# A graph network and expert kernel on one core: GpSimd takes over the whole split of level 0's weights

## The chip, the cores and the metric

One core of a Trainium2 chip. The time is that of one execution on the device, in microseconds (us).

## The reference

A graph network of three levels on 625 nodes of 256 features, followed by a layer of 8 experts. What matters here is the first of them:

```python
def _edge_conv(x, src, dst, W, b):
    xi = x[dst]
    xj = x[src]
    m = jnp.concatenate([xi, xj - xi], axis=-1) @ W + b
    s = jax.ops.segment_sum(m, dst, num_segments=N)
    cnt = jax.ops.segment_sum(jnp.ones((dst.shape[0],), m.dtype), dst, num_segments=N)
    return s / jnp.maximum(cnt, 1.0)[:, None]
...
for W, b in ((W0, b0), (W1, b1), (W2, b2)):
    h = jax.nn.relu(_edge_conv(h, src, dst, W, b))
    xs.append(h)
cat = jnp.concatenate(xs, axis=-1)
return cat @ Wf + bf
```

There are 20,000 edges, sorted by their target. x goes through a layernorm first. W has two halves: one for a node's own row (xi) and one for its neighbour minus itself. Since the sum over edges is linear, a level is (upper half of W minus lower half) applied to the own row times the node's degree, and the lower half applied to the neighbours' rows, added up through a 625 x 625 matrix of edge counts.

## The kernel before

One program writes out the instructions of each engine by hand, with semaphores between them. Five things run in its first 41 us.

**The matrix of edge counts.** The edges are taken in 40 units of 500. VectorE makes two tables of zeros and ones for each pair of units (`hot_pair`, lines 991 to 1004: `hot_lo` at L997 and `hot_key` at L1000, each comparing a constant table in SBUF with the edges' numbers in SBUF). TensorE multiplies them into a pane in PSUM (`sum_unit`, L1434 to L1444), and ScalarE copies each pane to its place in `a_hi` or `a_f` (`write_pair`, L724). Where a new pair of tables may overwrite an old one, VectorE waits for TensorE. TensorE's pairs of units are its `sum_pair(12)` to `sum_pair(38)`, with other products written in between them by hand (L1476 to L1508).

**The layernorm.** VectorE takes statistics of x (`bn_stats` L1013, `bn_aggr` L1016), ScalarE the square root, VectorE three Newton steps (L1024 to L1028), ScalarE writes the rows (`xn_row`, L739). TensorE transposes them (L1469), ScalarE rounds them to float32r (`ht_upper`, L746 to L750) and VectorE takes what rounding lost (`ht_lower`, L1046 to L1050).

**Level 0's weights.** W0 (two halves) and the first part of Wf are loaded to `w_stage` by SyncE (L485, L487). Every weight that a product uses is split into an upper half, rounded to float32r (`w_hi`), and a lower half, the rest (`w_lo`), so that three products give float32 precision (`exact3`, L1383). Parts 0, 1 and 2 are the neighbours' half, the difference of the two halves, and Wf's part. For level 0 VectorE makes the difference (L1036, in place), ScalarE the three upper halves (`w_upper`, L743) and VectorE the three lower halves (`w_lower`, L1041). The semaphore `w_split` counts 1 when parts 0 and 1 are there and 2 when part 2 is. TensorE waits for 1 before its first product with the weights (L1485, `ys_product`, L1406), together with `ht_ready`, and for 2 before the product with Wf at the end of level 0 (L1621). SyncE waits for 2 before it loads W1 into the same `w_stage` (L507).

**The later weights.** GpSimd makes the difference (L614) and the lower halves (L620) for level 1 with ScalarE's upper halves (L842), behind a wait for all additions of the adjacency (`a_added`, VectorE L1091) and for the load; for level 2 and the end it makes everything (`split_weights`, L574: difference L584, upper halves L587, lower halves L591). TensorE's levels 1 and 2 wait for counts 3 and 4 of `w_split` (L1615).

**GpSimd's queue** is: constants to L572; then a wait for `span_read` and `max_read` and four tiny operations on the ranges of the chunks (L603 to L606, `flagged`), which decide whether a general path is taken (not here); then a wait for all layernorm rows and a DMA that adds bf to x (L610); then the level 1 work.

SyncE's queue loads, in order, the edges, x, W0 and Wf's part, biases, the 16 blocks of expert weights, then (behind `w_split`) W1 and the rest.

Of the kernel before, what the change touches and what calls it, by code (L numbers as in the profile page):

```python
# [8 lines left out]
D = 256  # L9
# [84 lines left out]
def build(nc, x, src, dst, W, B, Wf, bf, Wg, bg, W1, b1, W2, b2, out):  # L94
    f32, f32r = mybir.dt.float32, mybir.dt.float32r
    bf16, i32, i16, u32 = mybir.dt.bfloat16, mybir.dt.int32, mybir.dt.int16, mybir.dt.uint32
    ALU = mybir.AluOpType
# [5 lines left out]
    with ctx:  # L103
        def sb(name, shape, dt, scope=ctx):
            return scope.enter_context(nc.sbuf_tensor(name, shape, dt))

        def sem(name):
            return ctx.enter_context(nc.semaphore(name))
# [35 lines left out]
        w_stage = sb("w_stage", [P, 3, KC, D], f32, gnn)  # L144
        w_hi = sb("w_hi", [P, 2, KC, 3 * D], f32r, gnn)
        w_lo = sb("w_lo", [P, 2, KC, 3 * D], f32r, gnn)
# [114 lines left out]
        w_in = [sem(f"w_in{l}") for l in range(LEVELS + 1)]  # L261
# [7 lines left out]
        w_split = sem("w_split")  # L269
# [16 lines left out]
        tables = sem("tables")  # L286
        base_ready = sem("base_ready")
        a_zeroed = sem("a_zeroed")
        w_diffed = sem("w_diffed")
        w_hi_done = sem("w_hi_done")  # L290
        w1_diffed = sem("w1_diffed")
        w1_hi_done = sem("w1_hi_done")
        hot_made = sem("hot_made")
# [179 lines left out]
        def edge_cols(a):  # L473

            return bank[3 + a][0:EP, 0:ET].rearrange("p (j q) -> p q j", j=EH)
# [63 lines left out]
        def _(pool):  # L539
# [34 lines left out]
            def split_weights(l):  # L574
# [15 lines left out]
                for i, part in parts:  # L590
# [5 lines left out]
                pool.sem_inc(w_split, 1)  # L596


            pool.wait_ge(span_read, 2)
            pool.wait_ge(max_read, 2)  # L600
            pool.wait_ge(consts, 5)
# [4 lines left out]
            pool.tensor_scalar(flags[:, 2 * CHUNKS - 2:], lo[:, SPLIT_CHUNK:SPLIT_CHUNK + 2], -1.0,  # L606
                               float(SPLIT - 1), ALU.mult, ALU.add).then_inc(flagged, 1)

            pool.wait_ge(xn_ready, NT)
            pool.dma_start(x_sb[:], bf.unsqueeze(0).unsqueeze(0).broadcast_to((P, NT, D)), accum_op=ALU.add)\  # L610
                .then_inc(bf_added, 16)
# [78 lines left out]
        def _(act):  # L690
# [26 lines left out]
            def chunk_starts(a):  # L717

                _, starts = nc.values_load_multi_w_load_instructions(
                    base_i[0:1, a:a + 8], engines=(mybir.EngineType.Activation,), min_val=0, max_val=NODES - 1,  # L720
                    skip_runtime_bounds_check_because="the least of a chunk's node numbers, which are below NODES")
                return starts

            def write_pair(g, a, starts):  # L724
                for k in (a, a + 1):
                    act.wait_ge(pane_done, k + 1)
                    if k >= 2:
                        act.wait_ge(a_written, k - 1)
                    act.copy((a_hi, a_f)[k % 2][:, :, ds(starts[k - a], TURN_W[g])],
                             pane(k).rearrange("p (n w) -> p n w", n=NT)).then_inc(a_written, 1)  # L730
# [9 lines left out]
                act.activation(xn[:, t, :], x_sb[:, t, :], ACT.Identity, bias=shift[:, t:t + 1], scale=rstd[:, t:t + 1])\  # L740
                    .then_inc(xn_ready, 1)

            def w_upper(i):  # L743
                act.copy(w_hi[:, 0, :, i * D:(i + 1) * D], w_stage[:, (1, 0, 2)[i], :, :]).then_inc(w_hi_done, 1)

            def ht_upper(i):  # L746
                (h, c) = Z_OUT[i]
                act.wait_ge(xn_t_done, i + 1)
                a, b = HALVES[h]
                act.copy(ht_hi[:, c, a:b], xn_bank(i)).then_inc(ht_hi_done, 1)  # L750
# [23 lines left out]
            write_pair(0, 6, starts[6:8])  # L774
            act.wait_ge(edge_col_done, 3)
            act.copy(edge_key[:].rearrange("p (q j) -> p q j", j=EH), edge_cols(1)).then_inc(edge_key_done, 1)
            act.wait_ge(w_in[0], 32)
            w_upper(0)
            starts = chunk_starts(8)
            write_pair(1, 8, starts[0:2])  # L780
            act.wait_ge(rstd_ready, 1)
# [4 lines left out]
            xn_row(2)  # L786
            write_pair(1, 14, starts[6:8])
            starts = chunk_starts(16)
            act.wait_ge(w_diffed, 1)
            w_upper(1)  # L790
            write_pair(1, 16, starts[0:2])
            xn_row(3)
            write_pair(1, 18, starts[2:4])
# [9 lines left out]
            ht_upper(2)  # L803
            ht_upper(3)
            write_pair(2, 28, starts[4:6])
            w_upper(2)
            write_pair(2, 30, starts[6:8])
            key_table(4)
            def write_units(g, u):
# [131 lines left out]
        def _(dve):  # L941
            n = [0]

            def mark(ins):
                n[0] += 1
                ins.then_inc(vec, 1)

            def wait_marked():
                dve.wait_ge(vec, n[0])

            def chain(ins):
                mark(ins)
                wait_marked()
# [61 lines left out]
            for t in range(NT):  # L1015
# [16 lines left out]
            dve.wait_ge(tables, 3)  # L1032
            dve.wait_ge(edge_col_done, 3)
            hot_pair(4)
            dve.wait_ge(w_in[0], 32)
            dve.tensor_tensor(w_stage[:, 0, :, :], w_stage[:, 0, :, :], w_stage[:, 1, :, :], ALU.subtract)\  # L1036
                .then_inc(w_diffed, 1)
            hot_pair(5)
            hot_pair(6)

            def w_lower(i):  # L1041
                dve.wait_ge(w_hi_done, i + 1)
                return dve.tensor_tensor(w_lo[:, 0, :, i * D:(i + 1) * D], w_stage[:, (1, 0, 2)[i], :, :],
                                         w_hi[:, 0, :, i * D:(i + 1) * D].bitcast(f32), ALU.subtract)

            def ht_lower(i):  # L1046
                (a, b), c = HALVES[Z_OUT[i][0]], Z_OUT[i][1]
                dve.wait_ge(ht_hi_done, i + 1)
                dve.tensor_tensor(ht_lo[:, c, a:b], xn_bank(i), ht_hi[:, c, a:b].bitcast(f32),
                                  ALU.subtract).then_inc(ht_ready, 1)  # L1050

            hot_pair(7)
            dve.wait_ge(tables, 4)
            w_lower(0)
            hot_pair(8)
            w_lower(1).then_inc(w_split, 1)
            ht_lower(0)
            ht_lower(1)
            hot_pair(9)
# [3 lines left out]
            hot_pair(11)  # L1063
            dve.wait_ge(tables, 5)
            hot_pair(12)
            w_lower(2).then_inc(w_split, 1)

            dve.wait_ge(flagged, 1)
            chain(dve.tensor_reduce(meta[:], flags[:], AX.X, ALU.max))
# [707 lines left out]
```

## Time and profile before

| | us |
|---|---|
| median of 3 runs | 165.92 (164.61 to 166.39) |
| the profiled execution | 165.11 |
| its span | 163.3 |
| TensorE, matmuls busy | 138.1 (85%) |
| VectorE busy | 88.6 (54%) |
| GpSimd busy | 65.6 (40%) |
| ScalarE busy | 63.8 (39%) |

The span is what the profiler saw of the core; about 1.8 us of the execution lie around it. PE is TensorE, PEld its loading of weights, DVE VectorE, ACT ScalarE, POOL GpSimd, SP SyncE; SPq and the like are an engine's queue. L12 is line 12 of the kernel. Busy shares are averages over stages that have different limits, so they don't tell what a change in one stage is worth. The spans of GpSimd instructions are rough. Names drop digits and buffer numbers (`w_stage`, `bank`). Consecutive instructions of an engine overlap a little in a timeline.

### The profile page before, as it was taken

What the parts mean: (1) busy time and instruction counts of PE and PEld (TensorE: products, weight loads), DVE (VectorE), ACT (ScalarE), POOL (GpSimd) and SP (SyncE); (2) the same over time, 40 slices, a digit from 0 to 9 for tenths busy, and PEclk for the clock granted to TensorE, in tenths of its full rate; (3) what the DMA queues carried; (4) which work ended last, traced back from release to release, by engine and by line L of the source; (5) the groups of instructions that cost most, each with busy time, mean ns of one, the idle gap of its engine ahead of it and who ended that gap; (6) DMA issues with size and microseconds to landing.
All of it is one profiled execution on the core that took longest, in us unless ns stands there. A gap on an engine that the chain in (4) does not pass through costs nothing.

```text
span 163.3 us, 3291 instructions
## 1 busy us (share of the span) xinstructions
PE 138.1 (85%) x1093; PEld 128.2 (79%) x1094; DVE 88.6 (54%) x251; ACT 63.8 (39%) x214; POOL 65.6 (40%) x78
## 2 busy tenths in 40 slices
PE   1432779998999999999999998887999999999800
PEld 1322659988998999999999987877999899999600
DVE  6799999789479980445048887641232223321110
ACT  7517895577172131322131480322443333333200
POOL 5805040000089099930000300058466867844531
PEclk9999999999999999999999999999999999999995
DMA  4959999799301910200000632012344434452322
GB/s 121 289 148 381 368 368 290 146 285 366 121 3 35 370 62 0 68 4 0 0 0 4 190 107 90 0 32 66 65 68 64 66 64 68 72 91 34 34 32 32
DMA packets 15770, 18.80 MB, mean 115 GB/s; under 512 B 1666, under 2 KB 13220, under 8 KB 15620
## 3 DMA queue, kind: packets, MB, share of 16 engines
q1 hardware_dynamic: 12692, 14.71, 27.8%
q0 software_dynamic: 3056, 3.80, 14.6%
q8 instruction: 13, 0.21, 0.6%
q14 instruction: 9, 0.07, 0.1%
HBM read 15.25 MB, written 3.26 MB: 113 GB/s over the span
## 4 chain that ended last, share of the span: by engine, by line
PE 73%; DVE 14%; issue 4%; DMA 3%; ACT 1%; POOL 1%; DVEq 1%; POOLq 0%; ACTq 0%
PE cnt_ps L1713 13%; PE bank L1699 8%; PE bank L1523 6%; PE g_ps L1699 6%; PE cnt_ps L1523 5%; PE g_ps L1387 3%; PE g_ps L1386 3%; PE g_ps L1388 3%; DVE hot_lo L997 3%; PE g_ps L1442 3%; PE bank L1442 3%; PE cnt_ps L1386 2%; PE bank L1386 2%; PE cnt_ps L1387 2%; PE cnt_ps L1388 2%
## 5 line engine op out<-in xcount | busy, mean ns | idle before, releaser
L660 POOL DMA_INDIRECT out_rows<-y_sb,row_of x13 | 20.6, 1585 | 15.9 <-SPq L533 9.1
L1331 DVE TENSOR_TENSOR y_sb<-cnt_ps,b_bc 128x256 f32<-128x256 f32 x13 | 5.5, 425 | 36.5 <-PE cnt_ps L1713 36.5
L1713 PE MATMUL cnt_ps<-w_sb,h_t 128*128 x104 | 24.7, 380 | 0.7 <-DVE y_sb L1331 0.7
L1713 PEld LDWEIGHTS cnt_ps<-w_sb,h_t 128*128 128x128 f32 x104 | 18.7, 190 | 3.1 <-issue 1.1
L654 POOL DMA_INDIRECT xg<-x_rows,row_of x11 | 12.9, 1176 | 18.7 <-DVE row_of L1364 15.7
L1699 PE MATMUL bank<-xt,w_fix 128*128 128x128 f32 x112 | 13.8, 276 | 1.2 <-DVE w_fix L1317 1.2
L1699 PEld LDWEIGHTS bank<-xt,w_fix 128*128 128x128 f32 x112 | 13.1, 191 | 2.2 <-DVE w_fix L1317 1.6
L911 ACT ACTIVATE h_t<-bank,b_col 128x128 f32<-128x128 f32 x28 | 8.0, 369 | 16.6 <-PE bank L1699 16.6
L997 DVE TENSOR_TENSOR hot_lo<-iota_lo,edge_rel 125x1024 bf16<-125x1024 int16 x20 | 13.8, 688 | 1.2 <-PE g_ps L1442 1.1
L1442 PE MATMUL bank<-hot_key,hot_lo 125*128 125x45 bf16 (+4 forms) x80 | 8.4, 245 | 5.5 <-DVE hot_key L1000 4.1
L911 ACT ACTIVATE h_t<-g_ps,b_col 128x128 f32<-128x128 f32 x24 | 6.9, 370 | 13.9 <-PE g_ps L1699 13.9
L1699 PEld LDWEIGHTS g_ps<-xt,w_fix 128*128 128x128 f32 x96 | 11.2, 192 | 0.9 <-issue 0.4
L1699 PE MATMUL g_ps<-xt,w_fix 128*128 128x128 f32 x96 | 11.8, 276 | 0.0
L1442 PEld LDWEIGHTS bank<-hot_key,hot_lo 125*128 125x128 bf16 x80 | 5.3, 125 | 8.0 <-DVE hot_key L1000 5.7
L614 POOL TENSOR_TENSOR w_stage<-w_stage 128x512 f32<-128x512 f32 x1 | 1.3, 1297 | 23.2 <-DMA w_stage<-in_L_gnn_Wf 23.2
L1442 PE MATMUL g_ps<-hot_key,hot_lo 125*128 125x45 bf16 (+4 forms) x80 | 8.5, 245 | 2.0 <-DVE hot_key L1000 1.8
L1317 DVE COPY w_fix<-w_sb 128x1024 f32 x13 | 9.2, 710 | 0.7 <-DVE in L1314 0.7
L1523 PE MATMUL bank<-a_hi,ys_hi 128*128 128x384 f32 (+1 forms) x30 | 9.1, 316 | 0.0
L1523 PE MATMUL bank<-a_hi,ys_lo 128*128 128x384 f32 (+1 forms) x30 | 9.0, 316 | 0.0
L1188 DVE SCALAR_TENSOR_TENSOR ut_lo<-bank,ut_hi 128x384 fp32r<-128x384 f32 x4 | 2.2, 558 | 12.5 <-ACT ut_hi L882 12.5
L762 ACT CAST ys_hi<-ys_f 128x256 fp32r<-128x256 f32 x10 | 4.1, 409 | 12.4 <-DVE ys_f L1084 12.4
L1000 DVE TENSOR_TENSOR hot_key<-key_tables,edge_rel 125x360 bf16<-125x360 int16 (+4 forms) x20 | 8.9, 445 | 0.0
(288 smaller groups left out, 379.0 us busy)
## 6 DMA issues: line engine op xcount, KB each, us to landing
w_sb<-in_L_ffn_W SPq DMA_DIRECT2D x16, 512.0 KB, 9.1
w_stage<-in_L_gnn_W SPq DMA_DIRECT2D x3, 512.0 KB, 4.8
w_stage<-in_L_gnn_Wf SPq DMA_DIRECT2D x4, 256.0 KB, 5.5
b_bc<-in_L_ffn_b SPq DMA_DIRECT2D x1, 1024.0 KB, 6.0
x_sb<-in_L_gnn_bf POOLq DMA_DIRECT2D x1, 640.0 KB, 15.0
x_rows<-x_f SPq DMA_DIRECT2D x1, 640.0 KB, 3.3
x_sb<-in_x SPq DMA_DIRECT2D x1, 512.0 KB
out_rows<-x_sb SPq DMA_DIRECT2D x1, 512.0 KB
```

Of the source, the lines that this page charges most:

```text
L654: pool.indirect_dma_start(out=xg[:, b, :], out_offset=None, in_=x2_rows, in_offset=bass.IndirectOffsetOnAxis(ap=rows, axis=0)).then_inc(x_ ...
L660: pool.indirect_dma_start(out=out, out_offset=bass.IndirectOffsetOnAxis(ap=rows, axis=0), in_=y_sb[:, b, :], in_offset=None, compute_op=AL ...
L911: last = act.activation(h_t[:, h, k, :], up_bank(h)[:, k * P:(k + 1) * P], ACT.Gelu, bias=b1_col[:, ds(e, 1), k:k + 1])
L997: dve.tensor_tensor(hot_lo[:, u % RING:u % RING + 2, :, :], iota_lo[0:EP].unsqueeze(1).broadcast_to((EP, 2, P, CT)), rel[:, 0].unsqueeze(2 ...
L1000: dve.tensor_tensor(hot_keys(u, 2), turn_keys(u // UNROLL)[0:EP].rearrange("p n w i -> p (n w) i").unsqueeze(1) .broadcast_to((EP, 2, NT * ...
L1317: dve.tensor_copy(w1_fix[:, h, :, :], w1_sb[:, ds(e, 1), :, :]).then_inc(w1_placed, 1)
L1386: pe.matmul(out_, lh, rh, start=first, stop=False, skip_group_check=True)
L1387: pe.matmul(out_, lh, rl, start=False, stop=False, skip_group_check=True)
L1442: last = pe.matmul(pane(k), hot_lo[:, u % RING, :, i], hot_keys(u)[:, 0, :, i], start=i == i0, stop=i == i0 + n_i - 1, skip_group_check=True)
L1523: step = pe.matmul(o, y[:, u, m], a_t[:, u, cols], start=first and u == 0 and y is y_parts[0], stop=u == NT - 1 and y is y_parts[-1], skip ...
L1699: last = pe.matmul(up_bank(h)[:, j * P:(j + 1) * P], w1_fix[:, h, k, j * P:(j + 1) * P], xt[:, k, h * P:(h + 1) * P], start=j == 0 and k == 0,
L1713: last = pe.matmul(bank[3][:, 0:D], h_t[:, h, k, :], w2_sb[:, ds(e, 1), k, :], start=k == 0, stop=k == HC - 1)
```

## The change

GpSimd makes the difference, the three upper halves and the three lower halves of level 0. Its new instructions stand between the constants and the four operations on the ranges (difference, parts 0 and 1), and between those and the DMA of bf (part 2). Each one waits for the one before it (`chain`). ScalarE's three copies and VectorE's four instructions go, with the two semaphores between them.

```diff
@@ gpsimd @@
+            def w_part(i):
+                return w_stage[:, (1, 0, 2)[i], :, :]
+
+            def w_lower(i):
+                return pool.tensor_tensor(w_lo[:, 0, :, i * D:(i + 1) * D], w_part(i),
+                                          w_hi[:, 0, :, i * D:(i + 1) * D].bitcast(f32), ALU.subtract)
+
+            pool.wait_ge(w_in[0], 32)
+            chain(pool.tensor_tensor(w_stage[:, 0, :, :], w_stage[:, 0, :, :], w_stage[:, 1, :, :], ALU.subtract))
+            for i in range(2):
+                chain(pool.tensor_copy(w_hi[:, 0, :, i * D:(i + 1) * D], w_part(i)))
+                chain(w_lower(i))
+            pool.sem_inc(w_split, 1)
             pool.wait_ge(span_read, 2)
             pool.wait_ge(max_read, 2)
...
+            chain(pool.tensor_copy(w_hi[:, 0, :, 2 * D:], w_part(2)))
+            chain(w_lower(2))
+            pool.sem_inc(w_split, 1)
             pool.wait_ge(xn_ready, NT)
@@ scalar @@
-            def w_upper(i):
-                act.copy(w_hi[:, 0, :, i * D:(i + 1) * D], w_stage[:, (1, 0, 2)[i], :, :]).then_inc(w_hi_done, 1)
-
...
-            act.wait_ge(w_in[0], 32)
-            w_upper(0)
...
-            act.wait_ge(w_diffed, 1)
-            w_upper(1)
...
-            w_upper(2)
@@ vector @@
             hot_pair(4)
-            dve.wait_ge(w_in[0], 32)
-            dve.tensor_tensor(w_stage[:, 0, :, :], w_stage[:, 0, :, :], w_stage[:, 1, :, :], ALU.subtract)\
-                .then_inc(w_diffed, 1)
             hot_pair(5)
             hot_pair(6)
-
-            def w_lower(i):
-                dve.wait_ge(w_hi_done, i + 1)
-                return dve.tensor_tensor(w_lo[:, 0, :, i * D:(i + 1) * D], w_stage[:, (1, 0, 2)[i], :, :],
-                                         w_hi[:, 0, :, i * D:(i + 1) * D].bitcast(f32), ALU.subtract)
...
             hot_pair(7)
             dve.wait_ge(tables, 4)
-            w_lower(0)
             hot_pair(8)
-            w_lower(1).then_inc(w_split, 1)
             ht_lower(0)
             ht_lower(1)
...
             hot_pair(12)
-            w_lower(2).then_inc(w_split, 1)
```

## Rows read from the trace of the kernel before

**Rows 1.** The page, part 2: busy tenths in 40 slices of 4.08 us.
```profile
PE   1432779998999999999999998887999999999800
DVE  6799999789479980445048887641232223321110
```

**Rows 2.** The chain of waits, 10 to 25 us: start us, us, what.
```profile
10.82 0.60 DVE hot_lo L997
...
14.67 0.74 DVE w_stage L1036
...
17.00 0.29 DVE hot_key L1000
...
21.29 0.56 DVE ht_lo L1049
...
24.74 0.37 PE bank L1386
```

**Rows 3.** Timeline of VectorE, 13 to 24.5 us; groups of ScalarE, 9 to 25 us.
```profile
14.59 0.82 DVE L1036 TENSOR_TENSOR w_stage<-w_stage 128x512 f32<-128x512 f32 x1
15.33 0.79 DVE L997 TENSOR_TENSOR hot_lo<-iota_lo,edge_rel 125x1024 bf16<-125x1024 int16 x1
...
16.32 0.68 DVE L997 TENSOR_TENSOR hot_lo<-iota_lo,edge_rel 125x1024 bf16<-125x1024 int16 x1
...
18.08 0.68 DVE L1043 TENSOR_TENSOR w_lo<-w_stage,w_hi 128x512 fp32r<-128x512 f32 x1
...
20.70 1.15 DVE L1049 TENSOR_TENSOR ht_lo<-cnt_ps,ht_hi 128x384 fp32r<-128x384 f32 x2 [0.39 <-ACT ht_hi L750]
...
L744 ACT CAST w_hi<-w_stage 128x512 fp32r<-128x512 f32 x3 | 1.9, 628 | 0.4 <-issue 0.4
```

**Rows 4.** Timeline of GpSimd, 12 to 24 us.
```profile
13.80 0.64 POOL L603 TENSOR_TENSOR over<-span_bc,limit 1x72 f32<-1x72 f32 x1 [5.98 <-issue]
14.52 0.34 POOL L604 TENSOR_TENSOR flags<-over,span_bc 1x72 f32<-1x72 f32 x1
...
20.61 1.76 POOL L610 DMA_DIRECT2D x_sb<-in_L_gnn_bf  x1 [4.44 <-ACT x_sb L740]
```

**Rows 5.** DMA issues, 0 to 14 us (last number: us to landing); SyncE's timeline.
```profile
w_stage<-in_L_gnn_Wf SPq DMA_DIRECT2D x1, 256.0 KB, 5.5
...
3.50 0.50 SPq L487 DMA_DIRECT2D w_stage<-in_L_gnn_Wf  x1
...
33.46 2.67 SPq L485 DMA_DIRECT2D w_stage<-in_L_gnn_W  x1
```

**Rows 6.** Timeline of GpSimd, 36 to 100 us.
```profile
45.61 1.30 POOL L614 TENSOR_TENSOR w_stage<-w_stage 128x512 f32<-128x512 f32 x1 [23.24 <-DMA w_stage<-in_L_gnn_Wf]
...
68.79 0.61 POOL L587 CAST w_hi<-w_stage 128x512 fp32r<-128x512 f32 x1
```

**Rows 7.** Timelines of VectorE and GpSimd, 49 to 66 us.
```profile
49.21 2.19 DVE L1188 SCALAR_TENSOR_TENSOR ut_lo<-z,ut_hi 128x384 fp32r<-128x384 f32 x2
...
49.39 1.60 POOL L620 TENSOR_TENSOR w_lo<-w_stage,w_hi 128x512 fp32r<-128x512 f32 x1
...
58.83 0.43 DVE L1078 TENSOR_TENSOR ys_lo<-ys_f,ys_hi 128x256 fp32r<-128x256 f32 x1
...
60.20 0.56 DVE L1078 TENSOR_TENSOR ys_lo<-ys_f,ys_hi 128x256 fp32r<-128x256 f32 x1 [0.19 <-ACT ys_hi L762]
...
65.21 0.56 DVE L1188 SCALAR_TENSOR_TENSOR ut_lo<-bank,ut_hi 128x384 fp32r<-128x384 f32 x1 [4.45 <-ACT ut_hi L882]
```

**Rows 8.** Timelines, 38 to 53 us; a stretch (its 1.00: granted clock); the chain.
```profile
38.57 4.11 DVE L1091 TENSOR_TENSOR a_hi<-a_hi,a_f 128x384 fp32r<-128x384 f32 x10
...
52.12 0.44 PE L1386 MATMUL bank<-ut_hi,w_hi 128*128 128x384 f32 x1 [0.22 <-issue]
...
24.50:30.80 6.30, 6.30 (x47) 6.02 (x46) 5.66 (x14) 3.59 (x18) 0.00 (x0) 1.00 0.99 240
...
27.06 0.21 PE cnt_ps L1387
...
32.75 0.12 PE cnt_ps L1387
```

More of the change, by code:

```diff
@@ L288, in build @@
         a_zeroed = sem("a_zeroed")
-        w_diffed = sem("w_diffed")
-        w_hi_done = sem("w_hi_done")
         w1_diffed = sem("w1_diffed")
```

## The prediction, made before the change was run

> **What bounds the kernel now.** The page comes first. Its digits by slice [rows 1] show TensorE low in the first six slices (0 to 24.5 us) and high later, and VectorE high from the start to 24.5 us: the change lies in the stretch where VectorE leads and TensorE waits. Who ends the waits is in the chain of waits, cut to 10 to 25 us [rows 2]: it runs along VectorE from hot_lo at 10.82 us to hot_key at 17.00, the difference of level 0's weights (14.67) among it, then over TensorE's transposes and ScalarE's ht_hi to VectorE's ht_lo (21.29), its next hot tables, and back to TensorE, which at 24.74 is in the first weight product. From there TensorE is dense. So a microsecond on VectorE before 20 us moves the start of the dense part by nearly a microsecond, and most of the span behind it is that dense part.
>
> **What goes.** VectorE loses four instructions. In its timeline [rows 3] the difference takes 15.33 - 14.59 = 0.74 us from start to start; the first lower half has 0.68, of which 0.08 overlaps its neighbour (14.59 + 0.82 against 15.33 is the same overlap), so 0.60; the second, of the same form, 0.60 too. These three stand ahead of ht_lo: 1.94 us. The third lower half stands behind the start of the dense part, where hot tables are made ahead of need: I value it at nothing, at most its 0.60 us. ScalarE loses three copies of 0.63 us [rows 3], two of them ahead of ht_hi. What ScalarE handles there (panes, layernorm rows) comes from VectorE's tables and scale, so I count no gain beyond VectorE's; but where VectorE gets faster, these 1.26 us keep ScalarE from being late in its place. VectorE waits 0.39 us for ht_hi ahead of ht_lo [rows 3]: so much of a gain, or of a loss, is swallowed there. With nothing else in play the first weight product would come 1.94 - 0.39 = 1.55 us earlier.
>
> **What comes, on GpSimd.** It has been idle for 5.98 us when its first flag operation starts at 13.80 [rows 4], so it is free from 7.8 us. The last part of W0's load is issued at 3.50 us and lands 5.5 us later, at 9.0 us [rows 5]; the wait wants all of it, so the work begins at 9.0. One difference or lower half alone takes 1.30 us, one copy to the upper half 0.61 us [rows 6]. Difference, upper 0, lower 0, upper 1, lower 1 are 3 x 1.30 + 2 x 0.61 = 5.1 us; the four waits on itself at some 0.1 us each (13.80 + 0.64 to 14.52 in rows 4 is such a gap) make 5.5 us: alone it ends at 14.5. TensorE asks for it at 24.5: as work it is well hidden. Behind it in GpSimd's queue stand four small flag operations, which only feed meta, read after VectorE's hot_pair(12); then upper 2 and lower 2 (2.0 us), wanted by the product with Wf at the end of level 0; then the DMA that adds bf, which waits for the last layernorm row anyway (20.61 [rows 4]) and whose result is read only after that product. None of these is near its user. SyncE waits for the second count of w_split before it loads W1, but its queue gets there only at 33.46 us [rows 5]; the count is then there in both kernels.
>
> **What it does to VectorE.** This term decides. The trace has one clean place where a GpSimd lower half meets VectorE instructions with two SBUF inputs: the two ut_lo at 49.21 [rows 7]. The form alone takes 0.56 us, a pair 2 x 0.56 - 0.08 = 1.04; here the pair took 2.19 us, and the lower half 1.60 in place of 1.30. The second ut_lo stood until GpSimd was done: 2.19 - 1.04 = 1.15 us for VectorE. A copy does the same, though the row shows only its tail: ys_lo at 60.20, behind a copy, took 0.56 us, the one at 58.83 took 0.43 [rows 7]. And in the very stretch of this change the tiny flag operations lengthened the difference (0.82 against 0.68 for the same form at 18.08) and hot_lo at 15.33 (0.79 against 0.68 at 16.32) [rows 3], and were stretched themselves: 0.64 and 0.34 us for one shape [rows 4]. hot_lo and hot_key read two SBUF inputs and follow each other without a gap: a GpSimd instruction gets in behind the running one, and the next stands for its time.
>
> In order: the difference (9.0 to 10.3) lies beside bn_stats, bn_aggr, a reduction and span_diag, which have one input tensor each and last to hot_lo at 10.82: nothing (if they do stand, 1.15 more). Upper 0 (10.4 to 11.0) reaches over 10.82: 0.2 us. Lower 0, between hot_lo and hot_key: 1.15. Upper 1, shorter than its duration by as much as the lower half: 0.61 - 0.15 = 0.46. Lower 1, at the Newton steps and hot_pair(3): 1.15. Upper 2 and lower 2, behind the flags and among hot_pair(5) to (8): 0.46 and 1.15. Sum 0.2 + 3 x 1.15 + 2 x 0.46 = 4.57 us of standing. Against it 1.94 saved and 0.39 swallowed: 4.57 - 1.94 - 0.39 = 2.24 us later at the first weight product. The bounds: below, no standing at all, a gain of 1.55; above, each instruction's whole duration and the difference too, 0.2 + 4 x 1.30 + 2 x 0.61 = 6.62, so 6.62 - 1.94 - 0.39 = 4.29 later. I take 2.24: ut_lo met exactly the instruction that is added, and the rows from 13.8 to 16 us show the same with hot_lo itself.
>
> The Trainium skill speaks against this change. In "SBUF — State Buffer", section "Who interferes with whom", it says that a VectorE instruction with two SBUF inputs contends with a GpSimd instruction that reads SBUF, and under "SBUF: two separate sides" that the loser is blocked for the whole instruction. The two ut_lo agree in kind; by whole durations in place of 1.15 and 0.46 the sum would be 0.2 + 3 x 1.30 + 2 x 0.61 - 1.94 - 0.39 = 3.0 us. The measured pair is what my sum goes by.
>
> **What the shift meets later.** The dense part moves as a whole. A gain would meet a gate: level 1 waits for the third count of w_split, given at 49.39 + 1.60 = 50.99 us [rows 7], and TensorE starts level 1 at 52.12 [rows 8]; GpSimd begins that work at 45.6, when W1's load has landed [rows 6], at the end of a full DMA queue. So 1.1 us of a gain pass at most. A delay finds that gate early: the other condition of the work, VectorE's last addition of the adjacency (38.57 + 4.11 = 42.68 [rows 8]), has 2.9 us to spare. The delay passes whole.
>
> TensorE's clock: the granted clock stands at 1.00 throughout [rows 8], but one step of a 256-column product takes 0.21 us at 27.06 and 0.12 at 32.75 [rows 8]: the pace of 1.2, then of 2.4 GHz. If the pace comes up at the same time of the run though the dense part begins 2.24 us later, 2.24 x (1 - 0.12 / 0.21) = 0.96 us are won back; if it falls out of step the other way, as much is lost. I take it in step.
>
> The profiled execution has 165.11 us, the median of the three shown 165.92. The sum on the first is 165.11 + 2.24 = 167.35; the forecast is for such a median, 165.92 + 2.24 = 168.2 us.
>
> **The rivals.**
> 1. VectorE's relief wins, which ends on the faster side: 165.92 - 1.1 = 164.8 us. Place: 9 to 20 us; it decides if the standing is below 1.94 us, under 0.4 for each of the five instructions that meet hot tables. For it: both relieved engines are busy there, and GpSimd has ten us to spare. Against it: the 2.19 us pair. Chance 0.10.
> 2. The standing is there but partly won back: TensorE's pace comes up at the same time, 168.2 - 0.96 = 167.2, or with 0.5 us more on instructions that read one tensor, 166.7 us. For it: VectorE has such instructions up to 10.8 us. Against it: hot tables are most of its time afterwards. Chance 0.25.
> 3. Heavier: whole durations, or GpSimd starting late. Its first tensor_tensor now comes at 13.80 behind idleness that the trace puts down to nothing ("issue"); if that hides something the engine needs, the difference too falls among the hot tables: 165.92 + 4.29 = 170.2 at worst, 168.9 by whole durations alone. Chance 0.17.
> The forecast as it stands has 0.48.
>
> **How the numbers follow.** A change within 1% (1.66 us) is about what a measurement of this kernel can't tell from none. The forecast lies 2.24 us above; of its 0.48 some 0.09 falls within 1%, of rival 2's 0.25 some 0.16, of rival 1 half (0.05; the other half if the gate lets more pass than I read), of rival 3 nothing. That makes faster 0.05, within 1% 0.30, slower 0.65. The range leaves out rival 1 and rival 3's far end: 165.9 to 169.9 us.
>
> **What would show it.** Right: GpSimd's difference starts near 9.0 us, ahead of the flags; in five places between 10.8 and 22 us a hot_lo of 0.68 or a small step behind a GpSimd instruction grows by 0.5 to 1.15 us; the first weight product starts near 26.8 us in place of 24.6, and what is behind it is later by the same. Wrong: hot_lo stays at 0.68 beside GpSimd's instructions and the product starts before 24.5 us (rival 1); the product is 2 us late but the span is not (rival 2: the pace, or slack behind that I didn't see); the difference starts after 10.8 us (rival 3). If W1's work or bf's DMA ended a wait on the path, my reading of the queues would be wrong.

## The result and the profile after

Twenty executions of each kernel: before 165.07 us in the median (164.25 to 166.41), after 166.00 (165.66 to 167.25). The ratio is 1.0058, 95% interval 1.0039 to 1.0076: slower by 0.93 us in the median, clear of noise, where 2.24 were forecast. The profiled execution of after has 165.9 us (span 164.1), that of before 165.11 (163.3). On another chip, timed again at the end, the same kernel gave 1.0085 (1.0053 to 1.0117). There the medians differ by 1.30 us. Both intervals hold 1.0053 to 1.0076. So the direction was right and the time lies in the range given, at its low end, but the size is less than half of the forecast's. (The forecast's base, 165.92, was the median of three executions and lies 0.85 above that of twenty, so the differences are what can be compared.)

The first weight product starts at 26.22 us in place of 24.55, 1.67 later. The page's part 2 of after, which answers to [rows 1], shows GpSimd busy in the third and fifth slices (8.2 to 12.2 and 16.3 to 20.4 us), where it did nothing in before, and VectorE about as busy as before, its standing counted as busy. The last row is before's:

```profile
PE   1413489998999999999999998897999999999800
DVE  6799999879659990346037887632222233321110
...
POOL 5886940000149279960000300057467766854531
```

```profile
POOL 5805040000089099930000300058466867844531
```

GpSimd's timeline of after, 8 to 24 us (start us, us, instruction), answers to [rows 4]:

```profile
8.68 1.26 POOL L605 TENSOR_TENSOR w_stage<-w_stage 128x512 f32<-128x512 f32 x1 [0.78 <-DMA w_stage<-in_L_gnn_Wf]
10.00 0.61 POOL L607 CAST w_hi<-w_stage 128x512 fp32r<-128x512 f32 x1
10.69 1.26 POOL L601 TENSOR_TENSOR w_lo<-w_stage,w_hi 128x512 fp32r<-128x512 f32 x1
12.02 1.33 POOL L607 CAST w_hi<-w_stage 128x512 fp32r<-128x512 f32 x1
13.42 1.26 POOL L601 TENSOR_TENSOR w_lo<-w_stage,w_hi 128x512 fp32r<-128x512 f32 x1
...
18.24 0.96 POOL L620 CAST w_hi<-w_stage 128x512 fp32r<-128x512 f32 x1
19.28 1.28 POOL L601 TENSOR_TENSOR w_lo<-w_stage,w_hi 128x512 fp32r<-128x512 f32 x1
```

VectorE's timeline of after over the same stretch answers to [rows 3]; the rows of before behind it show the small operations undisturbed:

```profile
10.12 0.51 DVE L1024 TENSOR_SCALAR var_eps<-mv 128x5 f32<-128x5 f32 x1
...
10.98 1.03 DVE L1026 TENSOR_SCALAR span_diag<-ident,span 80x80 f32<-80x80 f32 x1
...
12.54 0.33 DVE L1006 TENSOR_TENSOR hot_key<-key_tables,edge_rel 125x360 bf16<-125x360 int16 x1
...
13.00 0.36 DVE L1031 TENSOR_TENSOR newton<-rstd 128x5 f32<-128x5 f32 x1
...
13.59 1.11 DVE L1033 SCALAR_TENSOR_TENSOR rstd<-newton,rstd 128x5 f32<-128x5 f32 x1
...
16.92 0.82 DVE L1003 TENSOR_TENSOR hot_lo<-iota_lo,edge_rel 125x1024 bf16<-125x1024 int16 x1
...
18.65 0.77 DVE L1006 TENSOR_TENSOR hot_key<-key_tables,edge_rel 125x400 bf16<-125x400 int16 x1
19.34 1.77 DVE L1003 TENSOR_TENSOR hot_lo<-iota_lo,edge_rel 125x1024 bf16<-125x1024 int16 x1
...
22.39 1.14 DVE L1047 TENSOR_TENSOR ht_lo<-cnt_ps,ht_hi 128x384 fp32r<-128x384 f32 x2
```

```profile
10.05 0.17 DVE L1018 TENSOR_SCALAR var_eps<-mv 128x5 f32<-128x5 f32 x1
...
10.56 0.26 DVE L1020 TENSOR_SCALAR span_diag<-ident,span 80x80 f32<-80x80 f32 x1
...
11.81 0.17 DVE L1025 TENSOR_TENSOR newton<-rstd 128x5 f32<-128x5 f32 x1
...
12.21 0.17 DVE L1027 SCALAR_TENSOR_TENSOR rstd<-newton,rstd 128x5 f32<-128x5 f32 x1
```

Read the two engines side by side. `span_diag` starts at 10.98 and ends at 12.01, when the lower half that began at 10.69 is over (11.95). `rstd`, a 0.17 us operation, ends at 14.70, the second lower half at 14.68. `hot_lo` at 19.34 takes 1.77 us: it stands until the third lower half is over (20.56), then needs its 0.6. Each of these VectorE instructions begins under a GpSimd one and stands until that one ends. Not every one does: `bn_stats`, `bn_aggr`, the reduction and the reciprocal keep their durations beside GpSimd, and where a hot table is under way it can be GpSimd that is held: its copy at 12.02 takes 1.33 us in place of 0.61, while `hot_key` at 12.54 keeps its 0.33. VectorE's standing, over the durations of before: 0.34 + 0.77 + 0.19 + 0.94 = 2.24 us ahead of `hot_pair(4)`'s end and 0.42 + 1.09 = 1.51 behind it, 3.75 in all (4.57 forecast).

For what follows I take two points. P is the start of VectorE's instruction behind `hot_pair(4)`: 14.59 in before [rows 3], 16.92 in after. H is the start of the first `ht_lo`: 20.70 and 22.39. From H to the first weight product it is 3.83 to 3.85 us in all traces but one. So P is 2.33 later, P to H is 5.47 in place of 6.11, and the product is 2.33 - 0.64 = 1.69 later, as the row says within 0.02.

### The profile page after: what moved, and what is told of

It reads as the page before. It is cut to its first block, busy times and chain, and to the rows that moved or that the text cites. A ratio compares the mean times of both kernels' runs of the same rounds, so it can differ in the third digit from the quotient of the medians.

```text
span 164.1 us, 3293 instructions
## 1 busy us (share of the span) xinstructions
PE 137.1 (84%) x1093; PEld 127.6 (78%) x1094; DVE 89.9 (55%) x247; ACT 62.5 (38%) x211; POOL 72.5 (44%) x85
## 4 chain that ended last, share of the span: by engine, by line
PE 68%; DVE 22%; issue 4%; DMA 1%; ACT 1%; POOL 1%; DVEq 1%; POOLq 0%; ACTq 0%
PE cnt_ps L1708 14%; PE bank L1694 8%; PE g_ps L1694 7%; PE cnt_ps L1518 5%; PE bank L1518 4%; DVE hot_lo L1003 3%; PE g_ps L1381 3%; PE bank L1437 3%; PE g_ps L1382 3%; PE g_ps L1383 3%; PE g_ps L1437 2%; PE cnt_ps L1381 2%; DVE hot_key L1006 2%; PE bank L1381 2%; PE cnt_ps L1382 2%
## 5 line engine op out<-in xcount | busy, mean ns | idle before, releaser
L1708 PE MATMUL cnt_ps<-w_sb,h_t 128*128 x104 | 24.7, 380 | 0.7 <-DVE y_sb L1326 0.7
L668 POOL DMA_INDIRECT xg<-x_rows,row_of x11 | 12.1, 1104 | 18.7 <-DVE row_of L1359 15.7
L1003 DVE TENSOR_TENSOR hot_lo<-iota_lo,edge_rel 125x1024 bf16<-125x1024 int16 x20 | 14.9, 743 | 1.1 <-PE g_ps L1437 1.1
L628 POOL TENSOR_TENSOR w_stage<-w_stage 128x512 f32<-128x512 f32 x1 | 1.3, 1284 | 20.4 <-DMA w_stage<-in_L_gnn_Wf 20.4
L1006 DVE TENSOR_TENSOR hot_key<-key_tables,edge_rel 125x360 bf16<-125x360 int16 (+4 forms) x20 | 9.4, 470 | 0.0
L1437 PEld LDWEIGHTS g_ps<-hot_key,hot_lo 125*128 125x128 bf16 x80 | 6.0, 122 | 3.8 <-DVE hot_key L1006 3.2
```

The lines of the kernel that those rows point to most:

```text
L668: pool.indirect_dma_start(out=xg[:, b, :], out_offset=None, in_=x2_rows, in_offset=bass.IndirectOffsetOnAxis(ap=rows, axis=0)).then_inc(x_ ...
L1003: dve.tensor_tensor(hot_lo[:, u % RING:u % RING + 2, :, :], iota_lo[0:EP].unsqueeze(1).broadcast_to((EP, 2, P, CT)), rel[:, 0].unsqueeze(2 ...
L1006: dve.tensor_tensor(hot_keys(u, 2), turn_keys(u // UNROLL)[0:EP].rearrange("p n w i -> p (n w) i").unsqueeze(1) .broadcast_to((EP, 2, NT * ...
L1437: last = pe.matmul(pane(k), hot_lo[:, u % RING, :, i], hot_keys(u)[:, 0, :, i], start=i == i0, stop=i == i0 + n_i - 1, skip_group_check=True)
L1708: last = pe.matmul(bank[3][:, 0:D], h_t[:, h, k, :], w2_sb[:, ds(e, 1), k, :], start=k == 0, stop=k == HC - 1)
```

## The experiments

My theory after the result: it is GpSimd's reading of SBUF that makes VectorE stand, and the part of it ahead of P sets the product's lateness, while between P and H the work is not VectorE's alone. Rivals: GpSimd being busy at all is enough; the relief or the standing behind P counts too; the whole is an effect of when TensorE's pace rises. A table first; "product" and "span" are of the one trace, the ratio is against before on the same chip.

| kernel | P | P to H | product | span | ratio (95%) |
|---|---|---|---|---|---|
| before, two traces | 14.59, 14.68 | 6.11, 6.11 | 24.55, 24.63 | 163.3, 162.5 | |
| after, three traces | 16.92, 17.00, 17.55 | 5.47, 5.47, 5.49 | 26.22, 26.30, 26.88 | 164.1, 164.3, 164.5 | 1.0058; 1.0085 |
| reading instructions added | 16.54 | 6.89 | 27.14 | 164.9 | 1.0143 (1.0110 to 1.0175) |
| writing ones added | 14.94 | 6.11 | 24.89 | 164.0 | 0.9999 (0.9969 to 1.0029) |
| difference alone moved | 14.65 | 5.81 | 24.31 | 162.9 | 0.9990 (0.9969 to 1.0010) |
| part 2 given back | 17.19 | 5.49 | 26.52 | 163.9 | 1.0084 (1.0051 to 1.0117) |
| VectorE delayed | 16.99 | 6.09 | 26.93 | 164.8 | 1.0135 (1.0098 to 1.0172) |
| after, a copy's time on ScalarE | 17.15 | 5.81 | 26.80 | 164.6 | 1.0086 (1.0052 to 1.0120) |
| upper 0 and 1 early | 15.74 | 5.16 | 24.75 | 162.2 | 0.9979 (0.9954 to 1.0003) |
| the same, part 2 late | 14.66 | 5.18 | 23.67 | 162.7 | 0.9997 (0.9970 to 1.0025) |

### Seven GpSimd instructions added that read

Against before; the scratch tile is 128 x 2 x 512 and feeds nothing. They stand where the change puts its own.

```diff
+        scr = sb("scr", [P, 2, KC, D], f32, gnn)
...
+            chain(pool.memset(scr[:, 0, :, :], 1.0))
+            pool.wait_ge(w_in[0], 32)
+            def ex(short):
+                if short:
+                    chain(pool.tensor_copy(scr[:, 1, :, :], scr[:, 0, :, :]))
+                else:
+                    chain(pool.tensor_tensor(scr[:, 1, :, :], scr[:, 0, :, :], scr[:, 0, :, :], ALU.subtract))
+            ex(0)
+            for i in range(2):
+                ex(1)
+                ex(0)
             pool.wait_ge(span_read, 2)
...
+            ex(1)
+            ex(0)
             pool.wait_ge(xn_ready, NT)
```

> The kernel before, unchanged in what it computes, plus GpSimd work of the form and at the place of the change (four subtractions and three copies of 128x512, on a scratch tile, each waiting for the one before; one memset of 0.5 us ahead). VectorE and ScalarE keep all their instructions. Theory P (VectorE stands while GpSimd reads SBUF): nothing is saved, so the first weight product comes by the whole standing, 3.8 us in the changed kernel's trace, less VectorE's 0.39 us of slack: about 3.4 us after 24.55, and the time is 2.3 to 3.4 us longer. Rival Q (the time comes from GpSimd's own lateness: its flags and the DMA of bf behind the new work): the same lateness is there, so about 0.9 us longer, and hot tables of 0.68 us stay 0.68.

166.99 against 164.81 us, 1.0143. ScalarE and VectorE keep all their work here, so this is the price of GpSimd's instructions alone. VectorE's timeline:

```profile
11.99 0.79 DVE L1039 TENSOR_TENSOR newton<-rstd 128x5 f32<-128x5 f32 x1
...
13.01 0.46 DVE L1041 SCALAR_TENSOR_TENSOR rstd<-newton,rstd 128x5 f32<-128x5 f32 x1
...
13.59 1.53 DVE L1011 TENSOR_TENSOR hot_lo<-iota_lo,edge_rel 125x1024 bf16<-125x1024 int16 x1
...
18.27 1.09 DVE L1011 TENSOR_TENSOR hot_lo<-iota_lo,edge_rel 125x1024 bf16<-125x1024 int16 x1
19.29 1.20 DVE L1014 TENSOR_TENSOR hot_key<-key_tables,edge_rel 125x400 bf16<-125x400 int16 x1
```

Ahead of P it stands 1.95 us, behind it another 0.41 + 0.85. The product is 2.59 later, the median 2.2 to 2.4: nearly all of it arrives. The product was expected some 3.4 us late; P is only 1.95 later here, since the instructions met others than in after. Note also that P to H grows by 0.78 us (6.11 to 6.89): where VectorE keeps all its work, standing behind P does count.

### The same as instructions that only write

The kernel of the last run, with another `ex`: it fills as many bytes of the scratch tile as take about the same time.

```diff
+            def ex(short):
+                chain(pool.memset(scr[:].rearrange("p a k d -> p (a k d)").bitcast(bf16)[:, 0:(610 if short else 1390)], 1.0))
```

> As the run before it, but the seven instructions are memsets of about the same durations (1.26 and 0.6 us), which read nothing. Theory P: VectorE does not stand, the first weight product stays within 0.3 us of 24.55 and the time within 0.3 us of before. Rival Q: as late as with the instructions that read. If writing alone also blocks VectorE, both come out alike and P has to be widened from reads to any access.

164.56 us, 0.9999. GpSimd's timeline and a row of VectorE's, in order:

```profile
8.79 5.21 POOL L603 MEMSET scr<- 128x1390 bf16 x5 [0.39 <-DMA w_stage<-in_L_gnn_Wf]
...
12.85 0.68 DVE L1008 TENSOR_TENSOR hot_lo<-iota_lo,edge_rel 125x1024 bf16<-125x1024 int16 x1
```

GpSimd is busy from 8.79 to 14.0 us as in after, yet a hot table beside it takes its 0.68. A few small records look longer (`span_diag` 1.28), but what follows them isn't held: `hot_lo` starts at 10.97. P is 0.35 later, P to H unchanged, and the product 0.34 later, just outside the 0.3 expected; in time nothing shows. So it is the reading, as far as a memset is like the instructions that it stands for in all else. The Trainium skill, "SBUF — State Buffer", section "Who interferes with whom", says just this: a VectorE instruction with two SBUF inputs meets a GpSimd one that reads SBUF, not one that only writes. The traces agree: 1.53 us beside a reader, 0.68 beside a writer.

### The difference alone moved

```diff
+            pool.wait_ge(w_in[0], 32)
+            pool.tensor_tensor(w_stage[:, 0, :, :], w_stage[:, 0, :, :], w_stage[:, 1, :, :], ALU.subtract)\
+                .then_inc(w_diffed, 1)
...
             hot_pair(4)
-            dve.wait_ge(w_in[0], 32)
-            dve.tensor_tensor(w_stage[:, 0, :, :], w_stage[:, 0, :, :], w_stage[:, 1, :, :], ALU.subtract)\
-                .then_inc(w_diffed, 1)
```

> The kernel before with only the difference moved to GpSimd, at the place of the change (start near 8.7 us). ScalarE keeps the upper, VectorE the lower halves. Theory P: the difference lies beside bn_stats and bn_aggr, which did not stand in the changed kernel's trace; VectorE gains 0.74 us, the first weight product comes 0.35 to 0.75 us before 24.55 and the time falls by 0 to 0.7 us (TensorE's pace may keep part). Rival Q: no change or slower.

164.64 us, 0.9990. GpSimd's difference (8.96 to 10.22) makes nothing stand here: its neighbours are bn_stats and bn_aggr, and P is at 14.65. That hangs on when W0's load lands: where the difference ran later, `var_eps` met it and stood (0.26 us in one further trace of after, 0.72 in another, for 0.17; below). VectorE's row:

```profile
20.46 1.15 DVE L1049 TENSOR_TENSOR ht_lo<-cnt_ps,ht_hi 128x384 fp32r<-128x384 f32 x2 [0.70 <-ACT ht_hi L753]
```

VectorE saves 0.74 us and waits 0.70 in place of 0.39 [rows 3]: of the saving 0.30 remain at H (6.11 to 5.81; a `hot_key` beside the flags takes 0.12 more than in before). The product comes 0.24 earlier, less than the 0.35 to 0.75 expected. The other engines set H.

### After, with part 2 given back to ScalarE and VectorE

Against after. Parts 0 and 1 stay on GpSimd.

```diff
-            chain(pool.tensor_copy(w_hi[:, 0, :, 2 * D:], w_part(2)))
-            chain(w_lower(2))
-            pool.sem_inc(w_split, 1)
...
             write_pair(2, 28, starts[4:6])
+            act.wait_ge(w_in[0], 32)
+            act.copy(w_hi[:, 0, :, 2 * D:], w_stage[:, 2, :, :]).then_inc(w_hi_done, 1)
...
             hot_pair(12)
+            dve.wait_ge(w_split, 1)
+            dve.wait_ge(w_hi_done, 1)
+            dve.tensor_tensor(w_lo[:, 0, :, 2 * D:], w_stage[:, 2, :, :],
+                              w_hi[:, 0, :, 2 * D:].bitcast(f32), ALU.subtract).then_inc(w_split, 1)
```

> The changed kernel with part 2 (upper and lower half of Wf's part) given back to ScalarE and VectorE at their old places. Theory P: the standing behind GpSimd's last two instructions goes, 0.42 (hot_key) + 1.09 (hot_lo) = 1.51 us, so the first weight product comes at about 26.22 - 1.5 = 24.7 us, as in the kernel before, and the time is within 0.5 us of before. Rival Q: the last two instructions cost nothing, and the time stays some 0.9 us above before.

166.0 us, 1.0084: no better than after. VectorE's timeline:

```profile
18.93 0.35 DVE L1006 TENSOR_TENSOR hot_key<-key_tables,edge_rel 125x400 bf16<-125x400 int16 x1
19.20 0.68 DVE L1003 TENSOR_TENSOR hot_lo<-iota_lo,edge_rel 125x1024 bf16<-125x1024 int16 x1
...
20.63 0.69 DVE L1003 TENSOR_TENSOR hot_lo<-iota_lo,edge_rel 125x1024 bf16<-125x1024 int16 x1 [0.47 <-PE g_ps L1441]
...
22.68 1.15 DVE L1047 TENSOR_TENSOR ht_lo<-cnt_ps,ht_hi 128x384 fp32r<-128x384 f32 x2 [1.02 <-ACT ht_hi L759]
```

The 1.51 us of standing behind P are gone (0.35 and 0.68 again) and VectorE waits 0.47 + 1.02 = 1.49 instead; P to H stays at 5.49. The product was expected at 24.7 and starts at 26.52. So in the changed kernel, where VectorE has lost its own instructions there, the standing behind P costs nothing, and more relief of VectorE there brings nothing either.

### Before, VectorE delayed ahead of P

Two writes of the same scratch tile, behind `hot_pair(2)`.

```diff
             hot_pair(2)
+            for _ in range(2):
+                chain(dve.memset(scr[:], 1.0))
```

> The kernel before plus two memsets of a scratch tile on VectorE behind hot_pair(2), 1.8 us together; GpSimd has no new work. Theory A (a delay ahead of hot_pair(4) reaches the first weight product whole, and TensorE's pace comes up near 31 us of the run whenever the dense part began): first weight product 1.8 us after 24.55, pace up at 30.6 to 31.4 as in all five traces so far, the degree product about 1.2 later than 40.73, time 0.9 to 1.3 us longer. Rival B (the pace comes up a fixed stretch behind the start of the dense part, 6.3 us as in the kernel before): pace up at 32.7, time 1.8 us longer.

Two rows of 0.91 us, with the waits between them 2.4 us. P is 2.40 later, P to H 6.09, the product 2.38 later, the median 2.1 to 2.2 (1.0135 on some 165). A delay ahead of P passes to the product whole. The pace came up at 31.2 to 31.4 us, inside theory A's bounds and not at rival B's 32.7, yet the degree product is 1.77 later and the time is past A's 0.9 to 1.3 us, in part because the delay was 2.4 us in place of 1.8. So neither theory foretold both.

### After, with a copy's time on ScalarE

Against after; the write stands where ScalarE's second upper half stood.

```diff
             starts = chunk_starts(16)
+            act.activation(scr[:, 0, :, :].bitcast(f32r), ident[:, 0:1].unsqueeze(2).broadcast_to((P, KC, D)), ACT.Copy,
+                           scale=0.0)
```

> The changed kernel plus one ScalarE write of 0.6 us to a scratch tile at the place of the removed second upper half. Theory A (from hot_pair(4) to ht_hi the way leads through ScalarE's panes and layernorm rows, and VectorE has slack there): the first weight product comes 0.4 to 0.6 us after the changed kernel's 26.22, VectorE waits for ht_hi. Rival C (VectorE's hot tables set that stretch, as my prediction summed it): the product stays at 26.2.

ScalarE's and VectorE's timelines:

```profile
20.55 0.63 ACT L799 ACTIVATE scr<-ident 128x512 fp32r<-128x512 f32 x1 [0.41 <-issue]
...
22.96 1.15 DVE L1050 TENSOR_TENSOR ht_lo<-cnt_ps,ht_hi 128x384 fp32r<-128x384 f32 x2 [0.40 <-ACT ht_hi L762]
```

P to H goes from 5.47 to 5.81, and VectorE waits for ScalarE again. Of the copy's 0.63 us 0.34 count. With the 0.30 for the difference off VectorE that makes up the 0.64, and leaves nothing for ScalarE's first copy. (It is a sum of two runs and not a fixed price of each; see the next run.) In time the kernel can't be told from after (1.0086).

### Can the relief be had without the standing?

The difference on GpSimd, where it hurt nothing in the run above; upper halves 0 and 1 on ScalarE but early (one behind `write_pair(0, 2)`, one behind the square root); then also part 2's halves later (behind ScalarE's `write_rest(2, 22)` and VectorE's `hot_pair(14)`).

```diff
+            act.wait_ge(w_in[0], 32)
+            w_upper(0)
             act.wait_ge(var_ready, 1)
             act.activation(std[:], var_eps[:], ACT.Sqrt).then_inc(std_ready, 1)
+            act.wait_ge(w_diffed, 1)
+            w_upper(1)
```

> The kernel before with the difference on GpSimd (as in the run with the difference alone) and ScalarE's upper halves 0 and 1 taken out of its busy stretch into its idle time around 9 to 11 us. Theory A: 0.62 us goes from ScalarE's way, the first weight product comes at 23.6 to 23.8 against 24.31 with the difference alone; about half is given back by the pace, which still comes up near 31, so the time is 0.3 to 0.7 us below before. Rival C: nothing beyond the run with the difference alone (24.3).

> The kernel with the difference on GpSimd and ScalarE's upper halves 0 and 1 early, and in addition ScalarE's upper half 2 and VectorE's lower half 2 moved behind the start of the dense part, to places where those engines waited in the kernel before (27.2 and 30.0 us). Theory A: ScalarE's copy at 23.5 us stood between TensorE's unit 20 and unit 21 on the chain, so the first weight product comes up to 0.4 us earlier again; of it half is kept: time 0.4 to 1.0 us below before, interval clear of none. Rival C: no more than the run without this step (0.2% below before).

0.9979 (0.9954 to 1.0003) and 0.9997 (0.9970 to 1.0025): neither is clear of no change, though P to H fell to 5.16 and the second one's product started at 23.67, 0.88 earlier than in before. P to H is thus 0.65 shorter than with the difference alone (5.81), where after, which has neither copy on ScalarE, has 5.47. Where the last 0.3 us come from wasn't tested. (In the first one's trace all of VectorE's work up to P is 1.07 us late, from its wait for the load of `src_nat` on; less that, its product is at 23.68.) TensorE's and VectorE's timelines of the second:

```profile
44.25 0.84 PE L1514 MATMUL g_ps<-a_hi,ones_sq 128*128 128x256 f32 x5 [0.52 <-issue]
...
45.13 1.78 DVE L1176 TENSOR_TENSOR z<-z,g_ps 128x384 f32<-128x384 f32 x4 [4.01 <-PE g_ps L1514]
```

Level 1 starts at 51.41: the degree products came 1.54 earlier than in before (39.19 against 40.73), level 1 only 0.71. TensorE stood 0.52 us at 44.25, put down to nothing that the trace shows. So half of the gain is lost between the two points, and against the second trace of before (degree products at 40.13, level 1 at 50.96) all of it; these rows don't tell by what.

### Does TensorE's earlier work set its pace?

Before, with 36 small products that feed nothing between `sum_unit(5)` and `sum_pair(16)` (the expectation says 42; 36 stand in the kernel), and the first units handed out one by one.

```diff
+            sum_unit(4)
+            sum_unit(5)
+            keep_clock(10)
+            sum_unit(6)
+            sum_unit(7)
+            keep_clock(6)
...
             sum_pair(14)
+            keep_clock(6, 0)
             sum_pair(16)
```

> The kernel before plus 42 small products on TensorE between 12 and 21 us, put into its waits for hot tables, to a PSUM region that nothing else uses then. If what TensorE did before decides when its pace comes up, the pace is up at or soon after the first weight product (24.55), and the 6.3 us of dense work at the low pace shrink: time 1 to 3 us shorter. If the pace comes up at a set time of the run whatever TensorE did, it is up near 31 us and the time within 0.5 us of before.

Table of stretches (columns: stretch, its us, busy us of PE, PEld, DVE, ACT, POOL, granted clock, DMA share, GB/s):

```profile
12.00:18.00 6.00, 5.40 (x68) 4.53 (x68) 5.90 (x17) 4.38 (x18) 2.12 (x4) 1.00 1.03 370
18.00:24.50 6.50, 4.52 (x50) 3.25 (x51) 6.09 (x14) 5.85 (x26) 1.76 (x1) 0.87 1.08 360
24.50:29.60 5.10, 5.10 (x36) 4.91 (x36) 5.07 (x12) 2.94 (x15) 0.00 (x0) 0.50 1.14 282
29.60:33.00 3.40, 3.40 (x32) 3.19 (x30) 2.39 (x6) 2.16 (x9) 0.00 (x0) 0.99 1.01 130
```

The pace was up around 18 us, where the six transposes took 0.85 us in place of 1.52, and down again before the product, with a granted clock of 0.50 (1.2 of 2.4 GHz) until 29.6. The kernel is slower, 1.0139. Its trace also has a gap of TensorE up to 70.97 us, 1.60 us of waiting for VectorE's `ut_lo`, that before doesn't have and whose cause I didn't test, so this time says nothing on what an early pace would be worth.

### Both kernels traced again

> The kernel before again, for a second trace. First weight product within 0.4 us of 24.55. If the moment at which TensorE's pace comes up is bound to the engine's work it is again 6.3 us behind the product; if it is loose, somewhere between 27.9 and 31.4 us.

> The changed kernel again, for a second trace. Standing of VectorE ahead of hot_pair(4) of 2.0 to 2.5 us in all, first weight product 26.0 to 26.8; the pace comes up between 30.6 and 31.4 us as in the other late kernels, so the degree product is 0.9 to 1.3 us behind that of the kernel before.

> The changed kernel again, on another chip and in more rounds, with the question how much of the 1.67 us by which the first weight product is late reaches the end. Theory A (part of the delay is given back behind the product, because kernels with a late product leave TensorE's low pace sooner): 0.8 to 1.2 us over before, a ratio of 1.005 to 1.007 again. Rival B (the delay passes whole, and the first comparison was low): 1.5 to 1.8 us, a ratio of 1.009 to 1.011. Its trace should show the first weight product at 26.2 to 26.3 us by either; by A its low pace lasts some 4.4 us in each execution that is looked at, by B it can as well last the 6.3 us that one trace of before shows.

164.34 and 166.18 us for one execution each; then 166.01 against 164.71 in the median, 1.0085: between the bounds of the two theories on record. Chains of waits, before again and after (start us, us, what), answering to [rows 8]:

```profile
28.53 0.32 PE g_ps L1442 x4
28.85 0.15 PE cnt_ps L1386
29.00 0.12 PE cnt_ps L1387
```

```profile
29.58 0.21 PE cnt_ps L1383
...
30.74 0.12 PE cnt_ps L1382
```

TensorE's steps go at the high pace (0.12 us for a 256-column one, in place of 0.21) from 30.9 us on in one trace of before and from 28.8 in the other, with the product at 24.55 and 24.63: 2.1 us of difference that no instruction explains. The later rise costs 2.1 x (1 - 0.12/0.21) = 0.9 us by the arithmetic of rival 2; the traces differ by 0.60 at the degree products (40.73, 40.13) and 0.8 in span. The arithmetic asks too much: only the six product steps shorten (1.42 us in before, 0.76 in before again), while the panes of the edge matrix between them take 0.33 and 0.32 us at either pace.

The last kernel's trace shows that the standing isn't fixed either. Here W0's load landed later, GpSimd's difference ran at 9.57 (8.68 and 9.01 in the other two), and the instructions met others: `var_eps` the difference, `newton` and `hot_lo` the lower halves. VectorE:

```profile
10.14 0.72 DVE L1024 TENSOR_SCALAR var_eps<-mv 128x5 f32<-128x5 f32 x1
...
12.55 1.02 DVE L1031 TENSOR_TENSOR newton<-rstd 128x5 f32<-128x5 f32 x1
...
14.38 1.76 DVE L1003 TENSOR_TENSOR hot_lo<-iota_lo,edge_rel 125x1024 bf16<-125x1024 int16 x1
```

P is 2.96 later than in before, the product 2.33.

## Why the prediction was right in part, and where it was wrong

**The standing: right in kind and nearly in size.** It was priced from the pair of `ut_lo` at 1.15 us for a lower half and 0.46 for a copy. Ahead of P the prediction has 0.2 + 1.15 + 0.46 + 1.15 = 2.96 us; in the three traces P is 2.33, 2.41 and 2.96 later. What I had wrong is who stands: in the first trace no hot table ahead of P does. I cleared `span_diag` as an instruction with one input tensor, and there it stood for 0.77 us (0.09 in the other two); `var_eps` stood for 0.34, 0.09 and 0.55. The Trainium skill, "SBUF — State Buffer", section "Who interferes with whom", lists `tensor_scalar` among the operations that can take the port pair shared with GpSimd, and under "SBUF: two separate sides" has whoever comes second blocked for the whole instruction. The traces agree: both operations end where GpSimd's does. I had read that rule for two-input instructions only.

**The way to the product: right by two errors that cancel.** Behind P the prediction took off 1.94 saved and 0.39 swallowed and added 0.46 + 1.15 for part 2: 0.72 less. Measured were 0.64 less (6.11 to 5.47). But these are not the terms. Part 2's standing costs nothing in this kernel, as the one with part 2 given back shows by 1.49 us of waits, and VectorE's lower halves save nothing, since VectorE would only wait longer; by the runs the 0.64 are 0.30 for the difference and 0.34 for ScalarE's second copy, of which I had said "I count no gain beyond VectorE's". The product was forecast "near 26.8 us"; the traces have 26.22, 26.30 and 26.88.

**The step that failed: "The delay passes whole."** Of the 2.24 us forecast 0.93 came. On the first pair of traces 0.57 of the missing 1.31 us lie ahead of the product (1.67 late in place of 2.24), the larger part, 0.74, behind it, where the prediction took nothing off. The mean lateness of the product in after's three traces over before's two is 26.47 - 24.59 = 1.88 us; the spans differ by 164.3 - 162.9 = 1.4 us, the medians by 0.93 (20 executions of each) and by 1.30 on the second chip. Half a microsecond or more is missing at the end. Where it goes in these traces: the degree products are 1.65 later on the mean (42.08 against 40.43), level 1's start 1.46 (53.00 against 51.54), the span 1.4. The first part, 0.23, lies where TensorE's pace changes, which I took "in step". From the product to the first step at the high pace the kernels with a late product (after's three traces and those of the read, part 2, VectorE and ScalarE experiments) need 4.2 to 4.6 us; of before's two traces one needs 4.2, the other 6.3, as do the writing kernel and the one with the difference alone. So rival 2, a part won back, is nearest to what happened, but not by its rule of a fixed time: the rise lies anywhere from 27.9 to 31.4 us over all traces. The early kernels often have a long stretch at the low pace that the late ones were never seen to have. With one trace of each kernel I would have called 0.57 of the 1.67 us won back by the pace; the second trace of before takes all of that away, and only the medians say that something is. What sets the rise stays open, and so does what takes the rest. One rival was not tested: that the work taken off VectorE and ScalarE saves something behind the product. For it, the two kernels that keep all this work passed on more of their lateness (next paragraph); against it, their traces have 137.8 and 137.9 us from the product to the end of the span, and after's have 137.6 to 138.0.

**The rest.** The lateness that a delay brings at the end varies with it: 2.59 at the product gave 2.2 to 2.4 us, 2.38 gave 2.1 to 2.2, 1.97 and 2.25 gave 1.2 to 1.4, each with four executions and an interval of some 0.6 us to either side, so the difference is barely clear of noise. Of a gain nothing measurable came through, and of -0.88 at the product -0.05 to -0.13. The prediction had named the gate at level 1 for gains, but that isn't where it went: in that trace GpSimd's third count is given at 50.17 us and level 1 starts at 51.41. GpSimd's queue hurt nobody: bf's DMA is issued at 22.31 us against 20.61 [rows 4], by as much as the layernorm's last row is later, and level 1 starts at 52.68 behind GpSimd's lower halves (done at 52.00) without a wait. The third lower half and copy were rightly nothing up to the product: from H to the product it is 3.85 us with them and 3.83 without.

## What to carry to other kernels

Before work moves to GpSimd, go through VectorE's timeline under it one instruction at a time: whatever has two SBUF inputs, or is a small `tensor_scalar` on SBUF, can stand until GpSimd is done with the instruction that it is in (0.17 us of work took up to 1.1 us here); GpSimd's memsets, which only write, did no such harm. Who meets whom changed from trace to trace of one kernel. Take the path in pieces between two fixed points (here P and H), since work removed from an engine counts only in the pieces that it ends, and a saving elsewhere turns into a wait on the next engine. And trace the same kernel twice before you explain half a microsecond: two traces of the kernel before differed by 0.6 us at one instruction.

## What the runs showed of the hardware that I had not expected

- Operations of 0.17 and 0.26 us (`var_eps` on 5 elements a partition, `span_diag` on 80) were held for up to 0.55 and 0.77 us more by GpSimd, while `bn_stats`, `bn_aggr`, a reduction and a reciprocal beside it kept their durations.
- The pace of TensorE rose 3.1 to 6.3 us after the same product in traces of nearly the same kernels, with a granted clock of 1.00 shown in these stretches; only the kernel with extra products showed it at 0.50 while the pace was the same 0.21 us a step.
- More work of TensorE ahead of the dense part raised the pace early and lost it again.
